# Attention scores of a whole tile in one burst over four row groups, in place of two halves over two row groups each

## The chip, the cores and the metric

The kernel runs on one core of one Trainium2 chip. The metric is the device time in microseconds (us) from launch to end. All stretches below are counted from the first instruction of the profiled execution.

## What is computed

Input x is 64 x 256 x 192 (float32). A tower of two layers, then a mixture of experts:

```python
h = tok(x)                                  # pairs of tokens are pooled: 64 x 128 x 192
h = h + wkv_attention(layernorm(h))         # a recurrence over the 128 tokens of a row
h = h + mlp(layernorm(h))                   # 192 -> 768 -> 192, gelu
h = h + attention(layernorm(h))             # 12 heads of 16 channels, below
h = h + experts(layernorm(h))               # 8 experts, top 2, 192 -> 768 -> 192
# attention: q and k are layer-normed over 192 channels, then split into 12 heads
scores = einsum('bnqd,bnkd->bnqk', q, k) * scale
attn = softmax(scores, axis=-2)             # over the queries, for each key
o = einsum('bnqk,bnkd->bnqd', attn, v)
return o.reshape(b, l, d) @ Wo.T + bo + x
```

The softmax is over the queries. So the scores of a row of the batch lie in PSUM with the keys in the partitions and the queries in the columns, the maximum and the sum of a key are those of its partition, and the division by the sum goes into v.

## The kernel before

The 64 rows of the batch are 16 groups of 4 tiles (`G = 4`, a tile is one row of 128 tokens). The layers run as a software pipeline of rounds. In round i each engine handles several groups at once: stage `gn` (pooling of group i+1), `ga` (the recurrence), `gb` (residual and MLP), `gc` (q, k, v and the start of the attention), `gr` (the rest of the attention, and the router), `gs` (routing tables and the scatter to the experts). After the last round the expert part runs, which the change does not touch.

Nothing schedules the work at run time. Each engine has its own list, `round_`, written out by hand, and takes it in order. Semaphores tie the lists: an engine that waits holds back everything behind it on its own list. SyncE issues the loads and stores of the rounds (x, `hA_kept`, the output), GpSimd the small root operations and the scatter; both have lists of their own, which the change leaves alone.

The attention of one tile t of a group:

1. TensorE `c_queries(t)` (L761) transposes the queries into PSUM bank 7 (t = 0) or bank 3, ScalarE `c_queries` (L1075) copies them to `qT`.
2. TensorE `c_scores(t, half)` (L771, the matmuls are L783): 12 heads as 4 row groups of 32 partitions (j) times 3 column blocks (c). Row group j writes bank 4 + j. A half is two row groups, 6 matmuls, which the trace records as 12. Tile 0 waits for the keys `kT`. Every later tile waits for `exp_ready` of the same half of the tile before, because the banks are the same.
3. VectorE `c_max(t, half)` (L1545, the reduction is L1548) takes the negated maxima of the two banks of a half, 128 x 6 from 128 x 768.
4. ScalarE `c_exps(t, half)` (L1079, the activations are L1083) takes 6 exponentials with the sum of each, and raises `exp_ready`. `probs` has two buffers.
5. VectorE `c_values(t)` (L1553) waits for both halves, takes reciprocals of the sums (L1557) and scales v into `vpad` (L1558).
6. TensorE `c_values(t)` (L787, matmuls L799) multiplies `vpad` with `probs`, ScalarE `c_values` copies to `oT` (L1090, L1091), TensorE `c_project(t)` (L805, matmuls L812) waits for `oT` and, for t > 0, for `hF_ready` of the tile before, which VectorE `c_attn_add(t-1)` (L1572) raises.

What stands around these on the lists and counts below. TensorE: `b_mlp_down` (L708), `a_project` (L612, L615), `a_hidden` (transposes L585; it waits for the normalised rows and for `hB_ready`), `a_r` (channels_out with w_r, starts at L594; it waits for `xr_ready`), `a_k` and `a_v` (the same lines with w_k, w_v). VectorE: `b_mlp_add` (L1518), `a_residual` (L1507, raises `hB_ready`), `a_mix` (L1429 and six instructions of L1433, the first two of which are `xr`), `b_stats` (L1399, L1402 on `statsB`), `a_exponents`. ScalarE: `a_hidden` (L1028, copy to `hTA`), `ln_out` of group c (L963), `a_gate` (L1037).

On TensorE's list scores(0) stand between two parts of the MLP, scores(1, 0) ahead of `a_hidden` and scores(1, 1) behind it, scores(2, 0) ahead of `a_r` and scores(2, 1) behind it, and in the next round scores(3, 0) and scores(3, 1) each behind something and ahead of one `c_project`. On VectorE's list `b_stats` stands between c_max(2, 0) and c_max(2, 1).

Of the kernel before, what the change touches and what calls it, by code (L numbers as in the profile page):

```python
# [45 lines left out]
def build_tower(nc, a, out):  # L46
# [6 lines left out]
    G = 4  # L53
# [5 lines left out]
    HJ, HC = 4, HEADS // 4  # L59
# [21 lines left out]
    with ExitStack() as ctx:  # L81
# [467 lines left out]
        def _(pe):  # L549
# [105 lines left out]
            def a_k(g):  # L655
                pe.wait_ge(S["xk_ready"], g + 1)
                pe.wait_ge(S["tanh_r_ready"], g + 1)
                channels_out(0, w_k, w_k_diag, xk).then_inc(S["k_psum"], 1)
# [102 lines left out]
            def c_queries(g, t, gb=None):  # L761
                if t == 0:
                    pe.wait_ge(S["q_norm"], g + 1)
                    pe.wait_ge(S["kT_ready"], G * g + G)
                else:
                    pe.wait_ge(S["qT_ready"], G * g + t)
                    if gb is not None:
                        pe.wait_ge(S["hC_ready"], gb + 1)
                heads_transposed(7 if t == 0 else 3, qpad, t).then_inc(S["qT_psum"], 1)

            def c_scores(g, t, half):  # L771


                if half == 0:
                    pe.wait_ge(S["qT_ready"], G * g + t + 1)
                if t == 0:
                    pe.wait_ge(S["kT_ready"], G * g + G)
                else:
                    pe.wait_ge(S["exp_ready"], 2 * (G * g + t - 1) + half + 1)
                for c in range(HC):  # L780
                    for j in (2 * half, 2 * half + 1):
                        rows, heads = slice(32 * j, 32 * j + 32), slice(c * P, (c + 1) * P)
                        last = nc.tensor.matmul(ps[:, 4 + j, heads], kT[rows, t, heads], qT[rows, t % 2, heads],  # L783
                                                start=True, stop=True)
                last.then_inc(S["scores_psum"], 1)

            def c_values(g, t, gb):  # L787

                pe.wait_ge(S["vpad_ready"], G * g + t + 1)
                if t == 0 and gb is not None:  # L790
                    pe.wait_ge(S["hC_ready"], gb + 1)
                if t > 0:
                    pe.wait_ge(S["oT_ready"], G * g + t)

                for pairs in (range(0, 4), range(4, HEADS // 2)):
                    for odd in range(2):
                        for n in pairs:
                            rows = 32 * (n % 4)
                            last = nc.tensor.matmul(ps[rows:rows + 32, 2, n // 4 * P:(n // 4 + 1) * P],  # L799
                                                    vpad[:, t % 2, n, 32 * odd:32 * odd + 32],  # L800
                                                    probs[:, t % 2, 2 * n + odd, :],
                                                    start=(odd == 0), stop=(odd == 1))
                last.then_inc(S["oT_psum"], 1)
# [38 lines left out]
            def round_(i):  # L842
                gn, ga, gb, gc, gr, _ = stages(i)
                if gr is not None: c_queries(gr, 3, gc)
                if ga is not None: a_k(ga)
                if gr is not None: c_values(gr, 1, gc)
                if gr is not None: c_scores(gr, 3, 0)
                if gr is not None: c_project(gr, 0)
                if gr is not None: c_scores(gr, 3, 1)
                if gr is not None: c_project(gr, 1)  # L850
                if gr is not None: c_values(gr, 2, gc)
                if ga is not None: a_v(ga)
                if gc is not None: c_transposes(gc)
                if gr is not None: c_project(gr, 2)
                if gc is not None: c_qkv(gc, (0, 1))
                if gr is not None: c_values(gr, 3, gc)
                if gn is not None: a_delta(gn)
                if gr is not None: c_project(gr, 3)
                if gc is not None: c_qkv(gc, (2, 3))
                if gb is not None: b_transposes(gb)  # L860
                if gn is not None: a_scores(gn)
                if gb is not None: b_mlp_up(gb, 0)
                if gr is not None: r_transposes(gr, gc)
                if gb is not None: b_mlp_up(gb, 1)
                if gr is not None: r_logits(gr)
                if gb is not None: b_mlp_up(gb, 2)
                if gb is not None: b_mlp_up(gb, 3)
                if gr is not None: r_places(gr)
                if gb is not None: b_mlp_up(gb, 4)
                if gb is not None: b_mlp_up(gb, 5)  # L870
                if gc is not None: c_keys(gc, gr)
                if gb is not None: b_mlp_down(gb, (0,))
                if gb is not None: b_mlp_down(gb, (1,))
                if gc is not None: c_queries(gc, 0)
                if gb is not None: b_mlp_down(gb, (2,))
                if gc is not None: c_scores(gc, 0, 0)
                if gc is not None: c_scores(gc, 0, 1)
                if gb is not None: b_mlp_down(gb, (3,))
                if ga is not None: a_project(ga, gn)
                if gc is not None: c_queries(gc, 1, gb)  # L880
                if gc is not None: c_scores(gc, 1, 0)
                if gn is not None: a_hidden(gn)
                if gc is not None: c_scores(gc, 1, 1)
                if gc is not None: c_queries(gc, 2, gb)
                if gc is not None: c_values(gc, 0, gb)
                if gc is not None: c_scores(gc, 2, 0)
                if gn is not None: a_r(gn)
                if gc is not None: c_scores(gc, 2, 1)

            rounds(pe, round_)  # L890


# [445 lines left out]
        def _(dve):  # L1338
# [189 lines left out]
            def b_stats(g):  # L1528
                dve.wait_ge(S["hB_ready"], g + 1)
                ln_stats(g, "b", hB, statsB, mvB)  # L1530
# [117 lines left out]
            def round_(i):  # L1648
                gn, ga, gb, gc, gr, gs = stages(i)
                if gb is not None: a_reciprocal(gb, 0)  # L1650
                if gb is not None: a_reciprocal(gb, 1)
                if gb is not None: a_reciprocal(gb, 2)
                if gs is not None: r_pick(gs)
                if gb is not None: a_reciprocal(gb, 3)
                if gs is not None: r_place(gs)
                if ga is not None: a_tokens(ga)
                if gr is not None: c_keys(gr, 0)
                if gr is not None: c_keys(gr, 1)
                if gr is not None: c_keys(gr, 2)
                if gr is not None: c_keys(gr, 3)  # L1660
                if gb is not None: a_numerator(gb)
                if gb is not None: a_gate(gb)
                if gr is not None: c_max(gr, 0, 0)
                if gn is not None: a_delta(gn)
                if gr is not None: c_max(gr, 0, 1)
                if gc is not None: b_mlp_add(gc, gr)
                if gb is not None: a_residual(gb)
                if gr is not None: c_max(gr, 1, 0)
                if gr is not None: c_max(gr, 1, 1)
                if gr is not None: c_values(gr, 0)  # L1670
                if ga is not None: a_mix(ga)
                if gr is not None: c_max(gr, 2, 0)
                if gb is not None: b_stats(gb)
                if gr is not None: c_max(gr, 2, 1)
                if gr is not None: c_values(gr, 1)
                if gr is not None: c_max(gr, 3, 0)
                if gr is not None: c_attn_add(gr, 0)
                if gr is not None: c_values(gr, 2)
                if gr is not None: c_max(gr, 3, 1)
                if gr is not None: c_attn_add(gr, 1)  # L1680
                if ga is not None: a_exponents(ga)
                if gr is not None: c_attn_add(gr, 2)
                if ga is not None: a_fraction_args(ga)
                if gr is not None: c_values(gr, 3)
                if ga is not None: a_scan_p(ga)
                if gr is not None: c_attn_add(gr, 3)
                if ga is not None: a_scan_q(ga)
                if gc is not None: c_qk_stats(gc)
                if ga is not None: a_denominator(ga)
# [194 lines left out]
```

## Time and profile before

| | before |
|---|---|
| median of 3 runs | 1814.28 us (1808.73, 1814.28, 3801.61) |
| the profiled execution | 1804.56 us |
| its span, first to last instruction | 1802.4 us |
| mean granted TensorE clock | 0.924 |
| busy: TensorE matmul / VectorE / ScalarE / GpSimd | 88% / 75% / 66% / 41% |
| matmuls of the scores (L783) | 1536 records, the first at 174.2, the last at 1188.6 us |
| a round of the tower with every stage | 64.4 to 69.8 us |

A granted clock of 1 is 2.4 GHz, 0.5 is 1.2 GHz. In the timeline a row is a run of like instructions of one engine: start, duration, engine, line, operation, tiles, count, and in brackets how long the engine was idle before it and what ended that. Matmuls overlap, so one block's duration reaches a little over the start of the next; the time that a block costs TensorE is the distance to the start of the next.

### The profile page before, as it was taken

The numbers are of one execution on the slowest core, as the hardware profiler recorded it, in microseconds if no ns is written. First come the engines' busy times: TensorE is split into PE (matmuls) and PEld (weight loads), VectorE is DVE, ScalarE is ACT, GpSimd is POOL, SyncE is SP. The second block draws the span as 40 slices with busy tenths as digits, with TensorE's granted clock in tenths as the row PEclk, the third lists the DMA queues.
The fourth block names the chain that finished last, engine by engine and source line by source line (L and its number), as shares of the span: only waits on it lengthen the run. The fifth ranks groups of instructions, "written<-read, shape, count | busy, mean of one in ns | idle before, by whom it ended". The sixth has DMA issues, their size and how long they took to land.

```text
span 1802.4 us, 33505 instructions
## 1 busy us (share of the span) xinstructions
PE 1587.5 (88%) x10793; PEld 1232.4 (68%) x10793; DVE 1350.0 (75%) x2792; ACT 1191.8 (66%) x3269; POOL 743.2 (41%) x743
## 2 busy tenths in 40 slices
PE   3479999999999999999999988764999999999976
PEld 2246666666666676676676565543899999999876
DVE  4767787788778787788787643334999889989996
ACT  1246787787787787787787767544666666666643
POOL 0111232333333333234234122203567777777774
PEclk7789999999899999999998988656999999999998
DMA  4000010111011011011010000344677777677662
GB/s 118 27 27 18 19 51 27 43 51 38 30 50 41 27 50 44 24 50 47 21 54 35 13 34 25 101 147 146 167 182 168 160 162 163 158 165 170 160 156 60
DMA packets 121868, 145.39 MB, mean 81 GB/s; under 512 B 21074, under 2 KB 100419, under 8 KB 121795
## 3 DMA queue, kind: packets, MB, share of 16 engines
q1 hardware_dynamic: 92432, 113.00, 21.0%
q0 software_dynamic: 26592, 29.92, 9.0%
q10 hardware_dynamic: 2770, 1.56, 0.3%
q8 instruction: 38, 0.62, 0.1%
q14 instruction: 36, 0.29, 0.1%
HBM read 92.74 MB, written 46.77 MB: 77 GB/s over the span
## 4 chain that ended last, share of the span: by engine, by line
PE 69%; ACT 9%; DVE 8%; issue 5%; DMA 4%; POOL 3%; SPq 2%; POOLq 0%; DVEq 0%; ACTq 0%
PE ps L926 9%; PE ps L708 7%; PE ps L939 6%; PE ps L783 5%; PE ps L695 5%; PE ps L799 4%; PE ps L594 3%; PE ps L941 3%; PE ps L700 3%; PE ps L553 3%; PE ps L729 3%; PE ps L812 2%; PE ps L741 2%; ACT probs L1083 2%; DMA out<-ey,etoken 2%
## 5 line engine op out<-in xcount | busy, mean ns | idle before, releaser
L1322 POOL DMA_INDIRECT out<-ey,etoken x142 | 251.3, 1769 | 145.0 <-DMA out<-ey,etoken 50.1
L1083 ACT ACTIVATE probs<-ps,nmax 128x128 f32<-128x128 f32 x768 | 272.2, 397 | 24.1 <-DVE nmax L1548 24.0
L939 PE MATMUL ps<-w_hl,h_hi 128*128 128x384 f32 x852 | 253.7, 368 | 11.4 <-DVE ey L1823 11.4
L1195 ACT ACTIVATE h_full<-ps,eb 128x512 f32<-128x512 f32 (+1 forms) x234 | 158.7, 678 | 140.6 <-PE ps L926 140.5
L1548 DVE TENSOR_REDUCE nmax<-ps 128x6 f32<-128x768 f32 x128 | 121.6, 954 | 142.4 <-PE ps L783 142.4
L941 PE MATMUL ps<-w_hl,h_lo 128*128 128x192 f32 x852 | 215.9, 253 | 0.0
L1083 ACT ACTIVATION_READ_ACCUMULATOR probs<-ps,nmax 128x1 f32 x768 | 182.3, 237 | 0.0
L1312 POOL TENSOR_TENSOR w_lo<-w_raw,w_hi 128x1536 fp32r<-128x1536 f32 x39 | 156.1, 4003 | 40.1 <-ACT w_hi L1175 40.1
L939 PEld LDWEIGHTS ps<-w_hl,h_hi 128*128 128x128 f32 x852 | 163.5, 192 | 12.7 <-issue 9.7
L941 PEld LDWEIGHTS ps<-w_hl,h_lo 128*128 128x128 f32 x852 | 166.4, 195 | 0.0
L1783 DVE TENSOR_TENSOR h_lo<-h_full,h_hi 128x512 fp32r<-128x512 f32 (+1 forms) x234 | 150.1, 697 | 15.4 <-ACT h_hi L1196 15.2
L1196 ACT ACTIVATE h_hi<-ps,eb 128x512 fp32r<-128x512 f32 (+1 forms) x234 | 160.0, 684 | 0.0
L1290 POOL DMA_INDIRECT expert_rows_in<-rowR,slot_i x128 | 134.4, 1050 | 43.5 <-issue 41.5
L1246 POOL TENSOR_SCALAR shiftR<-mvR 128x4 f32<-128x4 f32 x16 | 19.9, 1241 | 310.4 <-DVE mvR L1582 310.4
L926 PE MATMUL ps<-x_hl,w_hi 128*128 128x512 f32 (+1 forms) x468 | 138.0, 376 | 10.7 <-DVE x_hl L1790 8.7
L783 PE MATMUL ps<-qT,kT 32*128 32x128 f32 x1536 | 123.6, 316 | 18.9 <-ACT qT L1077 12.3
L708 PE MATMUL ps<-w_down,hid 128*128 128x192 f32 x768 | 135.6, 330 | 1.4 <-ACT hid L1063 1.4
L926 PE MATMUL ps<-x_hl,w_lo 128*128 128x512 f32 (+1 forms) x468 | 136.0, 372 | 0.0
L783 PEld LDWEIGHTS ps<-qT,kT 32*128 32x128 f32 x1536 | 100.8, 210 | 47.7 <-issue 29.6
L708 PEld LDWEIGHTS ps<-w_down,hid 128*128 128x128 f32 x768 | 123.6, 190 | 5.9 <-ACT hid L1063 2.2
L695 PE MATMUL ps<-hTB,w_up 128*128 128x512 f32 x192 | 105.4, 663 | 15.6 <-ACT hid L1063 13.0
L1175 ACT ACTIVATE w_hi<-w_raw 128x1536 fp32r<-128x1536 f32 x39 | 59.0, 1513 | 76.6 <-DMA w_raw<-in_L_ffn_w 76.6
(292 smaller groups left out, 3704.0 us busy)
## 6 DMA issues: line engine op xcount, KB each, us to landing
w_raw<-in_L_ffn_w SPq DMA_DIRECT2D x39, 576.0 KB, 4.9
ex<-expert_rows_in SPq DMA_DIRECT2D x32, 528.0 KB, 5.4
w_raw<-in_L_ffn_w SPq DMA_DIRECT2D x39, 384.0 KB, 5.0
w_raw<-in_L_ffn_w SPq DMA_DIRECT2D x78, 192.0 KB, 5.5
xt<-in_x SPq DMA_DIRECT2D x16, 768.0 KB, 4.6
expert_rows_in<-xt SPq DMA_DIRECT2D x17, 528.0 KB, 7.0
hA_kept<-hA SPq DMA_DIRECT2D x16, 384.0 KB
out<-resC SPq DMA_DIRECT2D x16, 384.0 KB, 2.6
```

What stands on the lines that cost most here:

```text
L695: nc.tensor.matmul(ps[:, 2 + m % 2, :], w_up[:, m % 2, m * P:(m + 1) * P], hTB[:, m % 2, :], start=True, stop=False)
L708: last = nc.tensor.matmul(ps[:, 2 + t // 2, (t % 2) * C:(t % 2 + 1) * C], hid[:, m, t * T:(t + 1) * T], w_down[:, m, :], start=(m == 0), s ...
L783: last = nc.tensor.matmul(ps[:, 4 + j, heads], kT[rows, t, heads], qT[rows, t % 2, heads], start=True, stop=True)
L926: last = nc.tensor.matmul(ps[:, m % 4, 0:n_rows], w, x, start=(n == 0), stop=(n == len(terms) - 1))
L939: nc.tensor.matmul(ps[:, 4 + s, 0:2 * C], h_hi[b][:, m, q], w2_hl[b][:, m, :], start=(m == 0), stop=False)
L941: last = nc.tensor.matmul(ps[:, 4 + s, 0:C], h_lo[b][:, m, q], w2_hl[b][:, m, 0:C], start=False, stop=(m == FM - 1))
L1083: last = nc.scalar.activation(probs[:, t % 2, HJ * c + j, :], ps[:, 4 + j, c * P:(c + 1) * P], ACT.Exp, bias=nmax[:, t, j, c:c + 1], accum ...
L1195: nc.scalar.activation(h_full[:, m, 0:n], ps[:, m % 4, 0:n], ACT.Gelu, bias=eb1[u][:, m:m + 1])
L1196: nc.scalar.activation(h_hi[b][:, m, 0:n], ps[:, m % 4, 0:n], ACT.Gelu, bias=eb1[u][:, m:m + 1]).then_inc(S["e_hid"], 1)
L1312: nc.gpsimd.tensor_tensor(w1_lo[b][:, :, :], w1_raw[b][:, :, :], w1_hi[b][:, :, :].bitcast(F32), ALU.subtract).then_inc(S["w_low"], 1)
L1322: nc.gpsimd.indirect_dma_start(total, bass.IndirectOffsetOnAxis(ap=etoken[u][:, s:s + 1], axis=0), ey[b][:, s, :], None, bounds_check=NB * ...
L1783: nc.vector.tensor_tensor(h_lo[b][:, m, 0:n], h_full[:, m, 0:n], h_hi[b][:, m, 0:n].bitcast(F32), ALU.subtract).then_inc(S["e_hid_low"], 1)
```

## The change

`c_scores` loses its `half`: one call issues all 12 matmuls of a tile, for each column block over the four row groups in turn, and adds 2 to `scores_psum` at the end in place of 1 at the end of each half. For t > 0 it waits for `exp_ready` of both halves of the tile before. The calls on TensorE's list are merged and partly moved, `c_values(gr, 1)` goes ahead of `a_k(ga)`, and VectorE's list has each c_max(0, 1) and c_max(2, 1) directly behind its first half. ScalarE's list, the reductions, the exponentials and everything else stay.

```diff
-            def c_scores(g, t, half):
-                if half == 0:
-                    pe.wait_ge(S["qT_ready"], G * g + t + 1)
+            def c_scores(g, t):
+                pe.wait_ge(S["qT_ready"], G * g + t + 1)
                 if t == 0:
                     pe.wait_ge(S["kT_ready"], G * g + G)
                 else:
-                    pe.wait_ge(S["exp_ready"], 2 * (G * g + t - 1) + half + 1)
+                    pe.wait_ge(S["exp_ready"], 2 * (G * g + t))
                 for c in range(HC):
-                    for j in (2 * half, 2 * half + 1):
+                    for j in range(HJ):
                         rows, heads = slice(32 * j, 32 * j + 32), slice(c * P, (c + 1) * P)
                         last = nc.tensor.matmul(ps[:, 4 + j, heads], kT[rows, t, heads], qT[rows, t % 2, heads],
                                                 start=True, stop=True)
-                last.then_inc(S["scores_psum"], 1)
+                last.then_inc(S["scores_psum"], 2)
...
             def round_(i):          # TensorE
                 if gr is not None: c_queries(gr, 3, gc)
+                if gr is not None: c_values(gr, 1, gc)
                 if ga is not None: a_k(ga)
-                if gr is not None: c_values(gr, 1, gc)
-                if gr is not None: c_scores(gr, 3, 0)
+                if gr is not None: c_scores(gr, 3)
                 if gr is not None: c_project(gr, 0)
-                if gr is not None: c_scores(gr, 3, 1)
                 if gr is not None: c_project(gr, 1)
                 if gr is not None: c_values(gr, 2, gc)
...
                 if gb is not None: b_mlp_down(gb, (2,))
-                if gc is not None: c_scores(gc, 0, 0)
-                if gc is not None: c_scores(gc, 0, 1)
+                if gc is not None: c_scores(gc, 0)
                 if gb is not None: b_mlp_down(gb, (3,))
                 if ga is not None: a_project(ga, gn)
                 if gc is not None: c_queries(gc, 1, gb)
-                if gc is not None: c_scores(gc, 1, 0)
                 if gn is not None: a_hidden(gn)
-                if gc is not None: c_scores(gc, 1, 1)
+                if gc is not None: c_scores(gc, 1)
                 if gc is not None: c_queries(gc, 2, gb)
                 if gc is not None: c_values(gc, 0, gb)
-                if gc is not None: c_scores(gc, 2, 0)
                 if gn is not None: a_r(gn)
-                if gc is not None: c_scores(gc, 2, 1)
+                if gc is not None: c_scores(gc, 2)
...
             def round_(i):          # VectorE
                 if gr is not None: c_max(gr, 0, 0)
+                if gr is not None: c_max(gr, 0, 1)
                 if gn is not None: a_delta(gn)
-                if gr is not None: c_max(gr, 0, 1)
...
                 if gr is not None: c_max(gr, 2, 0)
+                if gr is not None: c_max(gr, 2, 1)
                 if gb is not None: b_stats(gb)
-                if gr is not None: c_max(gr, 2, 1)
                 if gr is not None: c_values(gr, 1)
```

## Rows read from the trace of the kernel before

**Rows 1.** The page: busy time of TensorE, and the chain that ended last

```profile
PE 1587.5 (88%) x10793; PEld 1232.4 (68%) x10793; DVE 1350.0 (75%) x2792; ACT 1191.8 (66%) x3269; POOL 743.2 (41%) x743
...
PE 69%; ACT 9%; DVE 8%; issue 5%; DMA 4%; POOL 3%; SPq 2%; POOLq 0%; DVEq 0%; ACTq 0%
```

**Rows 2.** Windows, one round each and one short stretch: length, busy, clock, DMA, GB/s

```profile
439.07:508.85 69.78, 66.93 (x478) 46.48 (x477) 51.87 (x129) 52.42 (x171) 22.93 (x34) 0.90 0.11 38
508.85:573.22 64.37, 61.04 (x478) 43.57 (x478) 51.76 (x129) 52.43 (x171) 22.62 (x34) 1.00 0.12 41
573.22:640.55 67.33, 64.12 (x479) 45.33 (x478) 51.86 (x129) 52.42 (x171) 22.73 (x34) 0.95 0.12 39
...
584.80:591.60 6.80, 6.80 (x44) 4.15 (x36) 6.06 (x16) 4.11 (x17) 5.49 (x5) 0.50 0.27 99
...
971.52:1041.02 69.50, 64.01 (x454) 43.81 (x453) 47.70 (x117) 50.76 (x166) 19.43 (x30) 0.90 0.08 28
```

**Rows 3.** Timeline of TensorE, the attention stretch of one round at full clock

```profile
508.85 1.27 PE L783 MATMUL ps<-qT,kT 32*128 32x128 f32 x24
510.06 2.22 PE L708 MATMUL ps<-w_down,hid 128*128 128x192 f32 x12
...
514.36 0.55 PE L741 MATMUL ps<-ident,qpad 128*128 128x128 f32 x3
515.56 0.94 PE L783 MATMUL ps<-qT,kT 32*128 32x128 f32 x12 [0.66 <-ACT qT L1077]
516.43 0.88 PE L585 MATMUL ps<-ident,hnA 128*128 128x128 f32 x6
517.58 0.94 PE L783 MATMUL ps<-qT,kT 32*128 32x128 f32 x12 [0.28 <-ACT probs L1083]
518.45 0.55 PE L741 MATMUL ps<-ident,qpad 128*128 128x128 f32 x3
520.11 1.07 PE L799 MATMUL ps<-probs,vpad 128*32 128x128 f32 x24 [1.11 <-DVE vpad L1558]
521.11 0.94 PE L783 MATMUL ps<-qT,kT 32*128 32x128 f32 x12
522.16 1.13 PE L594 MATMUL ps<-wkv,w_r 128*128 128x256 f32 x4
...
525.07 0.94 PE L783 MATMUL ps<-qT,kT 32*128 32x128 f32 x12
525.94 0.55 PE L741 MATMUL ps<-ident,qpad 128*128 128x128 f32 x3
526.32 1.03 PE L594 MATMUL ps<-wkv,w_k 128*128 128x256 f32 x4
...
529.12 1.07 PE L799 MATMUL ps<-probs,vpad 128*32 128x128 f32 x24
...
530.99 0.92 PE L812 MATMUL ps<-w_ao,oT 128*128 128x192 f32 x4
...
533.55 1.07 PE L799 MATMUL ps<-probs,vpad 128*32 128x128 f32 x24
```

**Rows 4.** Timeline of VectorE, the same stretch

```profile
515.00 0.92 DVE L1507 SCALAR_TENSOR_TENSOR hB<-ps,hA_kept 128x768 f32<-128x768 f32 x1
...
519.70 0.36 DVE L1558 TENSOR_TENSOR vpad<-v_s,rsums 128x192 f32<-128x192 f32 x1
...
524.16 0.94 DVE L1548 TENSOR_REDUCE nmax<-ps 128x6 f32<-128x768 f32 x1
525.03 1.12 DVE L1399 BATCH_NORM_STATS2 statsB<-hB 128x6 f32<-128x192 f32 x4
...
526.60 0.93 DVE L1548 TENSOR_REDUCE nmax<-ps 128x6 f32<-128x768 f32 x1
...
527.70 0.36 DVE L1558 TENSOR_TENSOR vpad<-v_s,rsums 128x192 f32<-128x192 f32 x1
```

**Rows 5.** Timeline of ScalarE, the same stretch

```profile
517.39 0.85 ACT L1028 ACTIVATE hTA<-ps 128x768 f32<-128x768 f32 x1
```

## The prediction

> **What bounds the kernel now.** I read the page first, then the windows of whole rounds, then the timelines of TensorE, VectorE and ScalarE over one attention stretch. The page says that TensorE is busy 88% of the span and carries 69% of the chain that ended last [rows 1]. The windows say the same of a single round: in the round from 508.85 to 573.22, all of it at full clock, TensorE is busy 61.0 of 64.4 us, VectorE 51.8 and ScalarE 52.4 [rows 2]. So a round ends when TensorE has gone through its list, and the two others have 12 us to spare, but not at every point. The timelines show where not: in the 25 us from the scores of tile 0 on, TensorE waits three times, 0.66 us for ScalarE's copy of the queries, 0.28 us for the exponentials and 1.11 us for vpad [rows 3]. There the attention's own chain (scores, maxima, exponentials, vpad, values) is as late as TensorE, and the kernel hides it by putting other blocks between the halves. I ask of each edit two things: how much issue time of TensorE goes, and what cover goes with it.
>
> **The issue time that goes.** A half of the scores costs TensorE 0.87 us (515.56 to 516.43, the start of a_hidden; 517.58 to 518.45). Tile 0, whose halves follow each other, costs 508.85 to 510.06, 1.21 us, for the same 24 records [rows 3]: the second half adds only 0.34, so the two halves already run beside each other there. A whole tile over four row groups should cost what one half costs, 0.87. It can't cost more than the 1.21 of the same 24 records, and hardly less than 0.87, since each row group still has three column blocks in turn. I take 0.87, as a half on two row groups is held up by its row groups' own sequence, the same for all four. Saved per group of four tiles: 0.34 for tile 0 and 0.87 for each of tiles 1 to 3, 2.95 us. If all of it counted, 16 groups would give 47 us.
>
> **Tile 1.** I replay the round that starts at 508.85. Scores(0) give 0.34: queries(1) start at 514.02 instead of 514.36. ScalarE's exponentials (0, 1) waited for these queries' copy, so they too end 0.34 earlier. Their old end is the release of scores(1, 1) at 517.58, and just behind it ScalarE's hTA copy at 517.39 [rows 3, 5]; the new end is about 517.2. In the old list scores(1, 0) and a_hidden filled this wait. Now a_hidden comes first and waits for hB, which VectorE ends at 515.92 [rows 4] (its list up to there hangs on the MLP's end and moves little): idle 514.4 to 516.0, some 1.5 us. It takes 0.8, then scores(1) wait for the exponentials, 0.4 us, run from 517.2 to 518.1, and queries(2) follow. Before, queries(2) stood at 518.45. TensorE is 0.34 ahead: of the 0.87 saved here nothing is left.
>
> The maxima lose more. c_max(1, 0) ran at 516.5, under the exponentials of tile 0. Now both maxima start when scores(1) are done, 518.2, and 0.87 + 0.87 later, at 519.95, VectorE turns to the reciprocals and vpad, 0.6 us more (528.06, the end of vpad(1), less 526.60 + 0.87 [rows 4]). Before, vpad(0) was ready at 519.70 + 0.36 = 520.06 [rows 4]. Now it comes at 520.6 and a_mix's xr, right behind it, some 0.5 later than before. ScalarE starts the exponentials (1, 0) 1.1 us later than before; they still end before TensorE next asks for them.
>
> **Tile 2 and a_r.** TensorE waits for vpad(0) from 518.5 to 520.6 (2.1 us, before 1.11), takes values(0) to 521.6, and then stands before a_r without scores(2, 0), which was the cover for xr (from 521.11 to 522.16 [rows 3]). It waits about 1.0 us and starts a_r at 522.65. a_r takes 2.91 (522.16 to 525.07), so scores(2) start at 525.56 and queries(3) at 526.43, against 525.94 before. TensorE is now 0.5 behind, and has spent the 0.34 of tile 0 and the 0.87 of each of tiles 1 and 2.
>
> **Values(1) ahead of a_k.** This is the large term. vpad(1) hangs on the whole VectorE sequence behind scores(2): before, c_max(2, 0) ran at 524.16, during a_r, then b_stats, c_max(2, 1) at 526.60, vpad(1) ready at 527.70 + 0.36 = 528.06 [rows 4]; TensorE spent this time in scores(2, 1), queries(3) and a_k, and came to values(1) at 529.12 without a wait [rows 3]. After the change nothing of it can start before scores(2) end at 526.5. From there: two maxima, 0.87 each; b_stats, 1.57 (525.03 to 526.60 [rows 4]); reciprocals and vpad, 0.6. Sum 3.9, vpad(1) at 530.4. TensorE is ready for values(1) at 526.8, because a_k (526.32 to 529.12, 2.80 us [rows 3]) now stands behind. It waits 3.7 us. Then values(1) 1.0, a_k 2.8, scores(3) at 534.3, project(0) at 535.2 against 530.99 before.
>
> **Tile 3.** Scores(3) are late enough that the exponentials (2, 1), which follow the maxima of tile 2 and end near 532.5, don't hold them. Saved is one half, 0.87, but project(1) wants hF of tile 0, and VectorE adds it only behind c_max(3, 0): 0.5 us of wait (the 0.87 of that maximum and the 0.3 of the add, less project(0)). Values(2) start at 537.4 instead of 533.55 [rows 3]: 3.9 us late.
>
> **Does the rest of the round take it back?** The waits of TensorE that are left in the round (for the hTC copy, for a gelu) are for copies of its own results, and move with it. VectorE and ScalarE have slack there and take none back. GpSimd's root for b_stats starts behind its scatter anyway and is needed 14 us later. SyncE's three transfers of a round wait for statistics and sums that move with the round. So a round is 3.9 us longer at full clock.
>
> **Sum at full clock.** 13 groups go through rounds with all these blocks: 13 x 3.9 = 51 us. In the last three a_r, a_k and at the end the MLP are missing; cover and waits both shrink, and I take 3 us each, 9 in all. Together 60 us.
>
> **The clock.** The round at full clock lasts 64.4 us; the one at 0.95 lasts 67.3 (2.9 more), that at 0.90 lasts 69.8 (5.4 more), and the nine rounds from 439.07 to 1041.02 average 66.9, 2.5 more [rows 2]. The granted clock is at 1.2 GHz from 584.80 to 591.60, which is 11.6 us into the round that starts at 573.22 [rows 2], just where the third wait of the attention stretch ends (520.11 is 11.3 us into its round [rows 3]). After the change the waits there grow from 2 us to 1.5 + 0.4 + 2.1 + 1.0 + 3.7 + 0.5 = 9 us. I expect the clock to fall in every round, once or twice: 2.9 to 5.4, with part of it under the wait for vpad(1). Taken: 3.9, 1.4 more than now, times 14, 20 us. The bounds are 0 and 2.9 more, 0 to 46 us.
>
> The Trainium skill ("TensorE: Matmul & The Clock Gate", Part 1: The HAM clock gate) says that the lowered clock is the default, and that an idle stretch takes the engine back to it. By that rule a wait as long as the one for vpad(1) should cost the clock in each round by itself. The trace of before has no tower wait so long, but it has falls behind much shorter ones, so the rule is, if anything, too mild here.
>
> **Total.** 1804.6 (the profiled execution's time; its span is 1802.4) + 60 + 20 = 1885 us. The median shown, 1814.3, and the lowest, 1808.7, are 10 and 4 above that execution; the forecast may be low by as much.
>
> **Rivals.**
> 1. *Every wait costs the clock* (0.15 of the chances). As above, but each round falls twice: 3.9 + 2.9 = 6.8 us a round, 16 x 6.8 = 109, 1914 us. For it: 9 us of waits in 30. Against: while TensorE waits, a lower clock costs nothing.
> 2. *The issue time counts* (0.04, the other side). If TensorE's list alone set the end, 2.95 x 16 = 47 us go: 1757 us. The point from which it decides: vpad(1) must be there when queries(3) are done, at 526.8, so its 3.9 us behind scores(2) would have to shrink below 0.3. What speaks for it is only TensorE's 88% and its 69% of the chain [rows 1]; the order of VectorE's list speaks against.
> 3. *Slack takes most of it back* (0.08). If later parts of the round absorb 2.5 of the 3.9 us and the clock stays as it is, 1.4 x 16 = 22 us, 1827 us. For it: VectorE and ScalarE have 12 us to spare. Against: TensorE has only 3.3 us idle in a round.
> 4. *Four row groups don't run beside each other fully.* At 1.21 a tile, 0.34 x 4 a round come on top, partly under waits: up to 20 us more. That is in the range, not apart.
>
> **How the numbers follow.** The forecast has 0.73, rival 1 0.15, rival 2 0.04, rival 3 0.08. Range: the low end has the full-clock sum with the last groups at nothing, 1804.6 + 51 = 1856, less 8 for errors of half a microsecond a round, 1848; the high end is rival 1's 1914. About what a measurement of this kernel can tell from no change is 2%, 36 us: slower by more 0.89, within 0.07, faster 0.04.
>
> **What would show it right or wrong.** In the timeline after: scores of every tile as one row x24 of about 0.87 us from start to next start; a wait of about 3.7 us ahead of the values matmul that follows queries(3), ended by vpad; about 2.1 us ahead of values(0), about 1 us ahead of a_r; rounds of 68 us where the clock is full, 71 to 73 in the mean, and a mean clock below 0.924. In the groups by line: the values matmuls with some 90 us idle before them (16 times 2.1 + 3.7), most of it ended by vpad. I am wrong if values(1) start without a wait, if rounds stay at 64 to 67 us, or if the scores keep 1.2 us a tile and the waits are short.

## The result and the profile after

The changed kernel takes 1878.57 us (median of 4 runs, 1876.2 to 1881.18), the kernel before 1815.7 beside it. The ratio is 1.0379, with a 95% interval from 1.0344 to 1.0414: 3.8% slower, where 1885 us was forecast. The median of before is taken over four executions, one of which took 3801.61 us, and the ratio leaves that one out, so it stands for some 69 us where the two medians differ by 62.9. The profiled execution took 1881.18 us, its span is 1879.0.

The page of the changed kernel, the lines that answer to [rows 1]:

```profile
PE 1555.9 (83%) x10793; PEld 1192.9 (63%) x10793; DVE 1343.5 (72%) x2792; ACT 1194.5 (64%) x3269; POOL 746.3 (40%) x743
...
PE 62%; DVE 11%; ACT 11%; issue 7%; DMA 4%; POOL 3%; SPq 2%; POOLq 0%; ACTq 0%; DVEq 0%
```

TensorE has fewer busy microseconds than before, 1556 against 1587, and holds less of the chain, 62% against 69%; VectorE and ScalarE have taken its place. That is the picture of an engine that has become faster and waits for others.

One round, by windows: the two short stretches are the ones at half clock, the last row is the whole round (length, busy times of TensorE, its weight loads, VectorE, ScalarE, GpSimd, then clock, DMA share, GB/s):

```profile
767.65:771.06 3.41, 3.28 (x10) 1.70 (x12) 2.19 (x5) 3.05 (x12) 2.62 (x3) 0.51 0.22 79
777.89:781.30 3.41, 3.41 (x16) 1.68 (x12) 0.00 (x0) 1.55 (x10) 0.88 (x2) 0.51 0.00 0
753.87:825.55 71.68, 61.47 (x478) 42.42 (x478) 51.70 (x129) 52.77 (x171) 22.66 (x34) 0.95 0.11 37
```

The round is 71.7 us long, against 64.4 at full clock and 66.9 in the mean [rows 2]. VectorE and ScalarE are as busy as before, 51.7 and 52.8. TensorE's timeline in the attention stretch of that round, to be laid beside [rows 3]:

```profile
753.87 0.95 PE L782 MATMUL ps<-qT,kT 32*128 32x128 f32 x24
754.75 2.22 PE L708 MATMUL ps<-w_down,hid 128*128 128x192 f32 x12
...
761.12 0.85 PE L585 MATMUL ps<-ident,hnA 128*128 128x128 f32 x6 [1.53 <-DVE hB L1502]
762.27 0.95 PE L782 MATMUL ps<-qT,kT 32*128 32x128 f32 x24 [0.30 <-ACT probs L1078]
763.15 0.55 PE L741 MATMUL ps<-ident,qpad 128*128 128x128 f32 x3
765.69 1.07 PE L798 MATMUL ps<-probs,vpad 128*32 128x128 f32 x24 [1.99 <-DVE vpad L1553]
767.78 2.08 PE L594 MATMUL ps<-wkv,w_r 128*128 128x256 f32 x4 [1.02 <-DVE wkv L1428]
...
772.15 0.95 PE L782 MATMUL ps<-qT,kT 32*128 32x128 f32 x24
773.03 0.55 PE L741 MATMUL ps<-ident,qpad 128*128 128x128 f32 x3
777.19 1.38 PE L798 MATMUL ps<-probs,vpad 128*32 128x128 f32 x24 [3.62 <-DVE vpad L1553]
778.51 2.07 PE L594 MATMUL ps<-wkv,w_k 128*128 128x256 f32 x4
...
782.68 0.95 PE L782 MATMUL ps<-qT,kT 32*128 32x128 f32 x24
783.56 0.92 PE L811 MATMUL ps<-w_ao,oT 128*128 128x192 f32 x4
785.06 0.89 PE L811 MATMUL ps<-w_ao,oT 128*128 128x192 f32 x4 [0.58 <-DVE resC L1567]
```

All 24 records of a tile cost TensorE 0.88 us (753.87 to 754.75), as half of them did before. The brackets are six waits of together 9.0 us, where [rows 3] have three of 2.05. The 3.62 us ahead of values(1) come back in thirteen rounds of the trace, with 3.61 to 3.63 us each time. VectorE and ScalarE behind scores(2) of the same round, the rows that release values(1) at 777.19 (first VectorE, then ScalarE):

```profile
773.16 1.82 DVE L1543 TENSOR_REDUCE nmax<-ps 128x6 f32<-128x768 f32 x2 [3.33 <-PE ps L782]
774.90 1.13 DVE L1394 BATCH_NORM_STATS2 statsB<-hB 128x6 f32<-128x192 f32 x4
...
776.71 0.36 DVE L1553 TENSOR_TENSOR vpad<-v_s,rsums 128x192 f32<-128x192 f32 x1
```

```profile
774.16 0.37 ACT L1078 ACTIVATE probs<-ps,nmax 128x128 f32<-128x128 f32 x1 [1.09 <-DVE nmax L1543]
...
776.76 0.28 ACT L1086 ACTIVATE oT<-ps 64x128 f32<-64x128 f32 x1
```

Vpad(1) is ready at 776.71 + 0.36 = 777.07. But ScalarE's copy of values(0) to oT, which values(1) also waits for, ends at 776.76 + 0.28 = 777.04. The profile names the later of the two; both are there, 0.03 us apart. The second experiment is about this.

Where the 76.6 us between the spans lie: 5.3 ahead of the first scores (they start at 179.5 instead of 174.2), 68.1 between the first and the last scores (to 1262.0, before to 1188.6), 3.2 behind. The change touches nothing ahead of the first scores, and the point moves by itself (one of the kernels below, run twice on one chip, has its first scores at 177.3 and at 179.5), so the 5.3 are not put down to it. 68 us arise where the change is.

### The profile page after: what moved, and what is told of

It reads as the page before. It is cut to its first block, busy times and chain, and to the rows that moved or that the text cites. A ratio compares the mean times of both kernels' runs of the same rounds, so it can differ in the third digit from the quotient of the medians.

```text
span 1879.0 us, 33475 instructions
## 1 busy us (share of the span) xinstructions
PE 1555.9 (83%) x10793; PEld 1192.9 (63%) x10793; DVE 1343.5 (72%) x2792; ACT 1194.5 (64%) x3269; POOL 746.3 (40%) x743
## 4 chain that ended last, share of the span: by engine, by line
PE 62%; DVE 11%; ACT 11%; issue 7%; DMA 4%; POOL 3%; SPq 2%; POOLq 0%; ACTq 0%; DVEq 0%
PE ps L921 8%; PE ps L708 7%; PE ps L934 6%; PE ps L695 4%; PE ps L594 4%; ACT probs L1078 4%; PE ps L782 4%; DMA out<-ey,etoken 3%; PE ps L700 3%; PE ps L936 3%; PE ps L553 3%; PE ps L798 3%; PE ps L729 2%; DVE nmax L1543 2%; PE ps L597 2%
## 5 line engine op out<-in xcount | busy, mean ns | idle before, releaser
L1078 ACT ACTIVATION_READ_ACCUMULATOR probs<-ps,nmax 128x1 f32 x768 | 172.4, 225 | 0.0
L798 PE MATMUL ps<-probs,vpad 128*32 128x128 f32 x1536 | 78.3, 300 | 89.1 <-DVE vpad L1553 82.6
L798 PEld LDWEIGHTS ps<-probs,vpad 128*32 128x32 f32 x1536 | 57.1, 117 | 107.8 <-DVE vpad L1553 51.8
L695 PE MATMUL ps<-hTB,w_up 128*128 128x512 f32 x192 | 99.7, 631 | 15.6 <-ACT hid L1058 13.0
```

The lines of the kernel that those rows point to most:

```text
L695: nc.tensor.matmul(ps[:, 2 + m % 2, :], w_up[:, m % 2, m * P:(m + 1) * P], hTB[:, m % 2, :], start=True, stop=False)
L1078: last = nc.scalar.activation(probs[:, t % 2, HJ * c + j, :], ps[:, 4 + j, c * P:(c + 1) * P], ACT.Exp, bias=nmax[:, t, j, c:c + 1], accum ...
```

## The experiments

The first four ran on a chip on which the kernel before takes 1812.6 us (median of 7), close to the 1815.7 beside the changed kernel. The others ran on a second chip, on which the kernel before takes 1876.5 and 1877.3. So those are read only by their ratio to the kernel before on the same chip; how that chip is slower stands at the end. The kernel before was not profiled there.

### a_k ahead of values(1) again

```diff
-                if gr is not None: c_values(gr, 1, gc)
                 if ga is not None: a_k(ga)
+                if gr is not None: c_values(gr, 1, gc)
```

> The changed kernel with one move taken back: a_k(ga) stands ahead of c_values(gr, 1) on TensorE's list again, as before the change. Theory (lost cover): a_k's 2.8 us run under the wait of 3.6 us that now stands before values(1), so that wait falls to about 0.9 us; scores(3) then come so early that the exponentials (2, 1) hold them by about 1 us. Net 1.7 us less in a round at full clock, 16 x 1.7 = 28 us, and up to 12 more from the clock: 1838 to 1852 us. Rival (what was lost lies in the whole-tile scores themselves, their waits for both halves of the exponentials and the later maxima, and the place of a_k is neutral): within 6 us of the changed kernel, 1873 to 1885.

Measured: 1841.56 us, ratio 1.0162 (1.0132 to 1.0192), 37 us less than the changed kernel. Its timeline of TensorE, a round at full clock:

```profile
616.93 0.55 PE L741 MATMUL ps<-ident,qpad 128*128 128x128 f32 x3
617.32 1.03 PE L594 MATMUL ps<-wkv,w_k 128*128 128x256 f32 x4
621.10 1.07 PE L798 MATMUL ps<-probs,vpad 128*32 128x128 f32 x24 [0.91 <-DVE vpad L1553]
623.07 0.95 PE L782 MATMUL ps<-qT,kT 32*128 32x128 f32 x24 [0.90 <-ACT probs L1078]
```

The 3.62 us have become 0.91, and the exponentials now hold scores(3) for 0.90, as the theory had it. The rival is out: this one line of order is more than half of the loss (the ratio falls from 1.0379 to 1.0162). The round from which the rows are has the full clock throughout and lasts 66.7 us, 2.3 more than the round of before at full clock. That is what whole-tile scores cost with a_k as cover.

### b_stats behind values(1), alone and with ScalarE's copy

```diff
                 if gr is not None: c_max(gr, 2, 1)     # VectorE
-                if gb is not None: b_stats(gb)
                 if gr is not None: c_values(gr, 1)
+                if gb is not None: b_stats(gb)
```

> The changed kernel with b_stats behind c_values(1) on VectorE's list. By the prediction's own step (vpad(1) alone releases values(1), and b_stats is 1.57 us of what it waits for): values(1) 1.5 us earlier in each round, 16 x 1.5 = 24 us, 1850 to 1858 us. Rival (two releasers: in the profile of the changed kernel vpad(1) is ready at 777.07 and ScalarE's oT copy of tile 0, queued behind the exponentials (2, 0), ends at 777.04, and values(1) starts at 777.19): the other one ends last and nothing moves, 1874 to 1884 us, with the wait before values(1) still 3.6 us, now ended by oT.

Measured: 1879.83 us, ratio 1.0371 (1.0339 to 1.0403), no change. TensorE's timeline:

```profile
772.76 1.07 PE L798 MATMUL ps<-probs,vpad 128*32 128x128 f32 x24 [3.52 <-ACT oT L1086]
```

Vpad(1) now comes 1.6 us ahead of need (771.18), ScalarE's oT copy ends at 772.71, and the wait is 3.52 instead of 3.62, ended by oT. The prediction's step failed this test: the chain that I had added up was right to the tenth, but it was one of two of the same length. The next kernel moves both:

```diff
+                if gr is not None: c_values(gr, 0)     # ScalarE
                 if gr is not None: c_exps(gr, 2, 0)
                 if gr is not None: c_queries(gr, 3)
-                if gr is not None: c_values(gr, 0)
```

> The second kernel of this call plus ScalarE's c_values(0) ahead of c_exps(2, 0), where ScalarE is idle. If values(1) has two releasers that come together, only both moves at once shorten the wait: values(1) about 1.5 us earlier, 20 to 30 us less than the changed kernel, 1848 to 1860 us. If b_stats alone is what counts, this equals the second kernel. If neither counts (a third releaser, such as the clock), all three stay at 1878.

Measured: 1859.85 us, ratio 1.026 (1.0222 to 1.0297), 19 us less than the changed kernel. b_stats alone leaves the wait as it is, both moves together shorten it. ScalarE's copy alone was not run; that it would not help either is argued from vpad(1), which is ready only at 777.07 in the changed kernel. The idle time of TensorE before the values matmuls, summed over the tower, by what ended it, for the changed kernel, for the one with b_stats moved and for the one with both moved:

```profile
L798 PE MATMUL ps<-probs,vpad 128*32 128x128 f32 x1536 | 78.3, 300 | 89.1 <-DVE vpad L1553 82.6 <-ACT oT L1086 6.5
```

```profile
L798 PE MATMUL ps<-probs,vpad 128*32 128x128 f32 x1536 | 77.1, 299 | 87.8 <-ACT oT L1086 55.7 <-DVE vpad L1553 32.0
```

```profile
L798 PE MATMUL ps<-probs,vpad 128*32 128x128 f32 x1536 | 82.3, 313 | 62.5 <-DVE vpad L1553 62.5
```

In the second the name changes and the sum stays; in the third the sum falls by 25 us. A name behind an arrow says who came last, not that its coming earlier would help.

### Four row groups against two pairs

```diff
-                for c in range(HC):
-                    for j in range(HJ):
+                for c, j in [(c, j) for h in range(2) for c in range(HC) for j in (2 * h, 2 * h + 1)]:
+                    if True:
```

> The changed kernel, with the 12 matmuls of a tile issued as 6 on row groups 0 and 1 and then 6 on row groups 2 and 3, as the two halves of tile 0 were before; the waits and the lists are those of the changed kernel. It tells what running four row groups side by side is worth. A tile should cost TensorE 1.21 us in place of 0.88, and its results come 0.34 later; since nearly every tile's scores now stand on the chain (maxima, exponentials, vpad), all four count: 4 x 0.34 = 1.36 us in a round, 16 x 1.36 = 22 us more, 1895 to 1912 us. Rival (the scores' own time is hidden, as waits follow them): within 6 us of the changed kernel.

Measured: 1917.02 us, ratio 1.0582 (1.0548 to 1.0616), 38 us more than the changed kernel. A tile's row of TensorE (start, duration):

```profile
555.35 1.27 PE L782 MATMUL ps<-qT,kT 32*128 32x128 f32 x24 [0.32 <-ACT probs L1078]
```

It spans 1.27 us instead of 0.95. So the four row groups do run side by side, and this is worth 0.32 us a tile in time to the result. The sum came out above its range, 38 instead of 17 to 34: 16 x 1.3 = 21 us are the four tiles. The other 17 us are not taken apart by a run, but they go with the clock: over the first thirteen rounds with scores, 13.7 us of a round are at half clock in the mean, where the changed kernel has 7.1 (over the span the mean clock is 0.894, against 0.922). The rival (hidden) is out.

### The wait for both halves alone, and the moves alone

The kernel before, with its halves in their places, but each waiting for both halves of the exponentials:

```diff
-                    pe.wait_ge(S["exp_ready"], 2 * (G * g + t - 1) + half + 1)
+                    pe.wait_ge(S["exp_ready"], 2 * (G * g + t))
```

> The kernel before, all lists and halves as they are, with one edit: a half of the scores of tile 1 to 3 waits for the exponentials of both halves of the tile before. It tells the price of the wait without the merge. Theory (the wait for both halves is a main part of the loss, since scores(t, 0) and its maxima no longer run under the exponentials (t-1, 1)): about 4 us a round at full clock, from tile 1 (scores(1, 0) held until 517.5 instead of 515.6) and tile 2 and 3 less; 1860 to 1885 us, about as slow as the changed kernel. Rival (the wait is cheap and the loss comes from the moved blocks, a_hidden, a_r and a_k without scores between them): under 15 us more than before.

Measured: ratio 1.0231 (1.0204 to 1.0257), 1919.13 us against 1876.5. The range given was for the other chip, 47 to 72 us above its 1812.6; 43 came. Its timeline of TensorE, at half clock:

```profile
773.12 1.65 PE L783 MATMUL ps<-qT,kT 32*128 32x128 f32 x12 [2.68 <-ACT probs L1083]
776.17 1.65 PE L783 MATMUL ps<-qT,kT 32*128 32x128 f32 x12
```

Scores(1, 0) wait 2.68 us for the exponentials, where [rows 3] have 0.66 for the queries, and a_hidden, which could run in a part of this time, stands behind them (in the changed kernel it starts 2.1 us behind queries(1), here 4.8 us). A part of the price is the clock: 16.5 us of a round are at half clock in the mean of the first thirteen, against 7.9 in the kernel below with tile 0 in one burst, on the same chip. Run again together with its counterpart:

> The wait for both halves of the exponentials alone, once more beside the moves alone, on the same chip. At full clock the replay gives 4.2 us a round, more than the moves (1.6) and about as much as the whole change (3.9): a ratio of 1.023 to 1.045. Rival (the moves cost more than the wait): below 1.015.

Measured: ratio 1.0217 (1.0176 to 1.0259). The counterpart has two of the moves of the change, with halves and their own waits:

```diff
-                if gc is not None: c_scores(gc, 1, 0)
                 if gn is not None: a_hidden(gn)
+                if gc is not None: c_scores(gc, 1, 0)
                 if gc is not None: c_scores(gc, 1, 1)
...
-                if gc is not None: c_scores(gc, 2, 0)
                 if gn is not None: a_r(gn)
+                if gc is not None: c_scores(gc, 2, 0)
                 if gc is not None: c_scores(gc, 2, 1)
```

> The kernel before with only the places changed: scores(1, 0) behind a_hidden and scores(2, 0) behind a_r, each directly ahead of its second half. Halves, their own waits and everything else stay. The counterpart to the run with the wait for both halves alone. Theory (scores(2, 0) behind a_r takes the cover from the wait for xr and starts the chain of tile 2 late, scores(1, 0) behind a_hidden matters little): 1.6 us a round at full clock, a ratio of 1.008 to 1.018. Rival (places without the wait are neutral, since the halves still overlap with the exponentials): 0.998 to 1.004.

Measured: ratio 1.0075 (1.0049 to 1.01). The idle time before the values matmuls is 66.7 us over the tower, 55.9 of it ended by vpad, against 26.3 before on the first chip and 34.8 in the kernel with tile 0 in one burst on this one:

```profile
L799 PE MATMUL ps<-probs,vpad 128*32 128x128 f32 x1536 | 95.8, 348 | 66.7 <-DVE vpad L1558 55.9 <-ACT oT L1091 9.3 <-issue 1.5
```

On this chip the wait costs about three times these two moves (by the intervals, between two and five times). All the rivals are out, though all the figures came in just under the lower ends of their ranges. The kernel with the moves alone has one round at full clock, which lasts 68.92 us, 4.6 more than [rows 2] have on the first chip where 1.6 was expected; 2.06 us of it are idle time ahead of a_k, next to this chip's own stall (at the end). The two kernels don't add up to the change: neither has values(1) ahead of a_k, which the first experiment shows to be the largest part, nor the burst over four row groups, nor the new order of VectorE's list. That the wait forces the moves (something must run in the meantime), and that they are cheap only with separate halves, is argued and not shown.

### What the merge is worth where no wait is added

Tile 0's scores wait for no exponentials. The kernel before with only these in one burst:

```diff
-                if gc is not None: c_scores(gc, 0, 0)
-                if gc is not None: c_scores(gc, 0, 1)
+                if gc is not None: c_scores_whole(gc, 0)
```

> The kernel before with only tile 0's scores issued as one burst over four row groups (tile 0 waits for no exponentials, and its halves already stood together). The merge without a new wait: 0.34 us a round less, 5 us in all, 1800 to 1812 us. Rival (the burst is worth nothing there, as VectorE and ScalarE are what tile 1 waits for): no difference.

Measured: 1868.35 against 1876.49 us, ratio 0.996 (0.9936 to 0.9985): 3 to 12 us, with 5 expected.

Then the same with VectorE's c_values(0) earlier:

```diff
                 if gr is not None: c_max(gr, 1, 0)
+                if gr is not None: c_values(gr, 0)
                 if gr is not None: c_max(gr, 1, 1)
-                if gr is not None: c_values(gr, 0)
```

> The previous kernel plus VectorE's c_values(0) ahead of c_max(1, 1). Theory: in the kernel before, TensorE's longest wait of a round, 1.11 us before values(0), is for a vpad(0) that stands behind the maximum of the second half of tile 1 on VectorE's list, though all that it needs has been ready since 517.5; ahead of it, vpad(0) comes 1 to 1.5 us earlier and that wait and the short one for xr go. 0.5 to 1 us a round at full clock, and the clock, which falls behind these waits, falls less often: 1770 to 1795 us. Rival (ScalarE, which then gets the maxima of (1, 1) later, passes the loss on): no change.

> Tile 0 in one burst and c_values(0) early, once more beside the run with the second edit alone, because the chip of the last call ran the kernel before 64 us slower than the chip of the first. Expected: a ratio of 0.98 to 0.99 if the chip is like the last one, 0.97 to 0.985 if it is like the first, where TensorE's list alone sets a round. Rival (the gain was taken from that chip's own stall): 0.995 to 1.0.

> The kernel before with one move: VectorE's c_values(0) ahead of c_max(1, 1); nothing is merged. It splits the gain of 1.2% of the kernel with both into its parts. Theory: the gain is nearly all from vpad(0) coming earlier, as tile 0's burst gives only 0.34 us a round: a ratio of 0.985 to 0.993 to the kernel before. Rival (the two need each other, since only with tile 0 in one burst do the maxima and the exponentials come early enough): 0.997 to 1.003.

Measured: both edits 0.9878 (0.9846 to 0.991) and, run again beside the second edit alone, 0.99 (0.9873 to 0.9928); values early alone 0.9943 (0.9918 to 0.9968). So each edit alone gives 0.4 to 0.6%, and together they give 1.0 to 1.2%, the sum. The first round with attention, which is at full clock in both, by windows, with both edits and then with the second alone:

```profile
169.45:232.95 63.50, 60.66 (x480) 43.25 (x478) 51.73 (x129) 52.42 (x170) 12.15 (x23) 1.00 0.08 26
```

```profile
167.51:231.33 63.82, 60.93 (x480) 43.56 (x478) 51.69 (x129) 52.42 (x170) 12.15 (x23) 1.00 0.08 26
```

They differ by 0.32 us, the 0.34 of tile 0. Against 64.37 [rows 2] they are 0.87 and 0.55 us shorter, but this round has no routing work yet. The next round at full clock of the kernel with both edits has it, and is no shorter than 64.37:

```profile
303.85:368.55 64.70, 60.83 (x479) 43.32 (x477) 51.87 (x129) 52.56 (x170) 23.00 (x34) 1.00 0.13 42
```

The 1.11 us before values(0) are gone from TensorE's timeline in both. The wait was for an operand whose inputs had been ready for 2 us (the exponentials of tile 0 by 517.58 [rows 3], vpad starts at 519.70 [rows 4]), behind a reduction that was not urgent. But 0.77 us of new idle time stand ahead of scores(2, 0), ended by ScalarE's copy of the queries, so that some 0.3 of the 1.11 are left as gain there.

One rival stays open: that a part of the gain comes out of this chip's own stall, a late tanh_r ahead of a_k. TensorE's idle time before a_k over the tower, with tile 0 in one burst alone and with both edits:

```profile
L594 PE MATMUL ps<-wkv,w_k 128*128 128x256 f32 x52 | 21.8, 562 | 34.8 <-ACT tanh_r L1046 33.1 <-issue 1.7
L594 PE MATMUL ps<-wkv,w_k 128*128 128x256 f32 x52 | 16.4, 446 | 11.8 <-ACT tanh_r L1046 11.8
```

It falls by 23 us, more than the 16 us between the two medians (1868.35 and 1852.28). With values early alone it is 36.9. So on this chip both edits together beat the kernel before by 1.0 to 1.2%; what they give on the first chip is not known, as they were not run there. The gain of values early was to be 0.7 to 1.5% and came in a little below.

### Whole tiles with lists made for them

```diff
+                if gr is not None: c_values(gr, 0)      # VectorE
                 if gr is not None: c_max(gr, 1, 0)
                 if gr is not None: c_max(gr, 1, 1)
-                if gr is not None: c_values(gr, 0)
...
+                if gr is not None: c_values(gr, 1)
                 if gr is not None: c_max(gr, 2, 0)
                 if gr is not None: c_max(gr, 2, 1)
                 if gb is not None: b_stats(gb)
-                if gr is not None: c_values(gr, 1)
...
+                if gr is not None: c_values(gr, 0)      # ScalarE
                 if gr is not None: c_exps(gr, 2, 0)
                 if gr is not None: c_queries(gr, 3)
-                if gr is not None: c_values(gr, 0)
```

> The changed kernel (whole tiles over four row groups) with the lists fitted to it: VectorE's c_values(0) ahead of both maxima of tile 1, c_values(1) ahead of both maxima of tile 2, and ScalarE's c_values(0) ahead of c_exps(2, 0). Each of them needs only exponentials that are long done. Theory: the waits before values(0) and values(1) go, and 0.5 us of a_r's; what stays is the wait for both halves of the exponentials before scores(1) and the loss behind it: 65.2 us a round at full clock, 1815 to 1830 us, about the kernel before. Rival (the whole-tile scores are slow in themselves): above 1850.

Measured: ratio 1.0 (0.9979 to 1.0022), a little better than expected. TensorE's idle time by group over the tower, values first, then scores, then a_r:

```profile
L798 PE MATMUL ps<-probs,vpad 128*32 128x128 f32 x1536 | 85.9, 323 | 8.7 <-ACT oT L1086 5.6 <-issue 1.9 <-DVE vpad L1553 1.2
L782 PE MATMUL ps<-qT,kT 32*128 32x128 f32 x1536 | 74.1, 327 | 52.3 <-ACT probs L1078 42.8 <-issue 9.0 <-ACT qT L1072 0.6
L594 PE MATMUL ps<-wkv,w_r 128*128 128x256 f32 x52 | 23.1, 591 | 41.1 <-issue 35.9 <-DVE wkv L1428 5.2
```

The 89 us before the values matmuls are down to 9. A part has only moved: 41 us stand ahead of a_r, where the changed kernel has 12. The profile gives most of it no name ("issue"), but in the round from 598.15 a_r starts at 612.42, just as VectorE's xr is due (two of the six instructions that run from 611.21 to 614.48), and xr now stands behind both maxima of tile 1. There are also 43 us for the exponentials, the price of the wait for both halves. The rival (whole tiles are slow in themselves) is out on that chip: with other lists they are level with the kernel before. These lists were not run with a_k moved as well, nor on the first chip.

## Why the prediction was right

- *What bounds.* Right: TensorE's list sets the round, and it hides the attention's chain between 508.85 and 534. The chain of after shows the exchange, TensorE from 69% down to 62%.
- *Issue time.* Right: 0.88 us a tile for 0.87 assumed; the two pairs, at 1.27, show that the concurrency is real. So, by 2.95 us for each of 16 groups, some 47 us of issue time did go, and were paid back in waits.
- *The waits.* Forecast 1.5 + 0.4 + 2.1 + 1.0 + 3.7 + 0.5; measured 1.53 + 0.30 + 1.99 + 1.02 + 3.62 + 0.58. The sum is 9.2 (put as 9 in the forecast) against 9.04.
- *The release of values(1).* This step was half right. The place, the size and vpad were as forecast, but I had followed VectorE's list alone. ScalarE's oT copy, behind six exponentials, was as late. The forecast's total didn't suffer; a remedy built on it failed.
- *A round at full clock.* The round of 71.68 us has a_r at 4.37 (767.78 to 772.15) and values(1) with a_k at 5.49 (777.19 to 782.68), where [rows 3] have 2.91 and 3.80. This is 3.15 us for the clock, which leaves 68.5 as an estimate of the round at full clock, 4.2 more than before; 3.9 was forecast. No round of the trace has the full clock throughout, so it can't be read off.
- *The clock.* Mis-sized. I took 1.4 us a round more than before; it is 3.15 against 2.5, 0.65 more. The clock does fall twice in each of the first thirteen rounds, and the mean clock is just below that of before (0.922, 0.924), as put down in advance. From the second of these on, each fall lasts 3.4 us. Before, a round had between none and 13.7 us at half clock, 5.5 in the mean of the first thirteen, against 7.1 now. The Trainium skill ("TensorE: Matmul & The Clock Gate", Part 1: The HAM clock gate) has an idle engine go back to the lower clock. After the wait of 3.62 us the trace agrees, with a clock of 0.51 in the row from 777.89; but so it is in the row from 767.65, behind waits of 1.99 and 1.02 us. And the round of the first experiment from which the rows are has waits of 1.52, 0.30, 1.99 and 1.01 us at the same places and keeps the full clock. So the length of a wait alone does not tell here whether the clock falls.
- *The total.* The forecast of 1885 us is 6 above the median. It was counted from the profiled execution of before, though, which lies 11 us below the median of before. As a difference, 80 us were forecast; 62.9 came by the medians, 69 by the ratio, and 76.6 by the two profiled spans, of which 68.1 lie in the tower. The thirteen rounds from the first scores on took 866.8 us before and 932.5 after, 5.05 more each, where 5.3 were forecast; in the round taken apart above, two size errors lie in opposite directions, 0.3 for the round and 0.75 for the clock. The larger miss is the last three groups. They were put at 9 us without a row behind it, and took 147.6 us before and 150.0 after, 2.4 more. So the forecast was 12 us too high for the tower, and that the total still came within 6 us is in part luck: 8.5 us arose outside the tower, where none were forecast.
- *Rivals.* Rival 1 (1914) had the two falls right and their price wrong (5.4 us a round at half clock, where 3.15 came). Rival 2 (issue time counts) is refuted by the six brackets, rival 3 (1.4 us a round in all) by rounds that are 5.05 us longer.

## What to carry to other kernels

When engines run hand-written lists, a block is also a cover. Before merging two halves, write down what stands between them and which wait it hides; here some 3 us of issue time a round went, and the waits grew by 7. When a wait is to be removed, look for every operand of the waiting instruction, since the profile names only the last. And look in front of a late operand for work of its own engine that is not urgent: one line moved gave 0.6% on the second chip, while the whole change cost 3.8% on the first.

## What was not expected

The same kernel takes 1812.6 us on one chip and 1876.5 on another, 3.5% more. In the waits of ScalarE and VectorE on the second chip there are lines that the first has not (kernel with tile 0 in one burst):

```profile
ACT tanh_r L1046 <- remote: 62.4, 12, 5.5
DVE nmax L1557 <- remote: 36.3, 16, 8.4
```

ScalarE stands idle up to 5.5 us ahead of tanh_r, 12 times, and TensorE then waits for tanh_r ahead of a_k. In one round tanh_r starts at 829.47, 4.9 us after the end of the last matmul that it waits for. Neither the profiles of the kernel before and of the changed one nor the first four experiments have such a line; all eight profiles of the second chip have one for nmax, and six of the eight have one for tanh_r; the two with the wait alone have none for tanh_r. The profile gives no cause ("remote"), and no run here was made to find it. The stall lies beside the stretch that the change touches and can hide a part of a loss there, which may be why the wait alone and the whole tiles with better lists came out cheaper than expected on that chip. The changed kernel itself was not run on the second chip.

The rounds of the changed kernel are nearly alike: the first with scores lasts 72.2 us, the next twelve 71.4 to 71.8, with the half clock at nearly the same two places each time (13.7 to 14.2 and 23.9 to 24.4 us into the round). Before, the first thirteen were 64.4 to 69.8 us, with the fall in different places or none.
